# The shared expert's first matmuls, moved from the end of the expert loop to its middle, in a fused Mamba and mixture-of-experts layer

## The chip, the cores and the metric

The kernel runs on all 8 cores of one Trainium2 chip, one of the eight sequences on each, and the cores do not talk to each other. The metric is the device time of the slowest core in microseconds (us). Before the change it is 4697.62 us, the median of two runs (4684.04 and 4711.21).

## The reference

For each token row x (8 sequences of 4096 tokens, 1024 features) the layer computes

```python
xn = layernorm(x)
s  = mamba(xn)          # in_proj, causal conv, selective scan with 16 states, gate branch z, out_proj
g  = silu(moe(xn))      # 8 experts, top 2 by a sigmoid gate, plus one shared expert
out = x + s * g

# inside moe(xn)
h      = gelu(einsum('bsd,edh->bseh', xn, W1) + b1)          # experts, hidden width 512
y      = einsum('bseh,ehd->bsed', h, W2) + b2
shared = gelu(xn @ Ws1 + bs1) @ Ws2 + bs2                    # the same two steps, every token
return einsum('bse,bsed->bsd', gate_full, y) + shared

# inside mamba(xn): the recurrence over time
h_t = exp(delta_t * A) * h_{t-1} + delta_t * x_t * B_t
y_t = sum_n h_t[n] * C_t[n] + D * x_t
```

## The kernel before, in words

Each core walks over its sequence in 16 chunks of 256 tokens (`T = 256`). Features lie on partitions, tokens along the free dimension. Every weight matrix is turned to bf16 once in HBM; the weights of the experts, of in_proj, conv and out_proj are streamed in again for every chunk. Only the shared expert's weights stay in SBUF (`ws1_b`, `ws2_b`).

A small class, `Sched`, collects operations in program order, gives each to an engine, and derives the semaphore waits from named buffers that operations read and write. It reorders nothing: each engine does its own operations in the order in which the loop at the end of `build_nc` emits them. So the place of a call in that loop is its place in every engine's queue.

What belongs to the change:

- `scan_group(i, g)`, lines 804 to 842, does one eighth of the channels. VectorE multiplies u by B (`dBx`, L810). ScalarE computes 16 exponentials (`dA`, L817) into 7 slots, VectorE does 16 scans (`h_b`, L827), and frees a slot with each. Then VectorE multiplies by C (L839). ScalarE can be at most 7 exponentials ahead of the scans.
- `idents_phase(i, g)` sums the 16 states with 16 matmuls by an identity and one by a diagonal of D, into PSUM bank P7, and ScalarE copies the result to `y_b` (L866).
- `ffn_expert(i, e)` loads 2 x 512 KB of W1 and does 32 matmuls into banks P4 and P5 (`P<-xn_b,sb_w`). Four ScalarE activations with Gelu empty them into `scrb2` (L914).
- `hgate_phase(i, e)` multiplies by the gate on VectorE (L924).
- `ffn_w2(i, e)` loads 2 x 512 KB of W2 and does 32 matmuls into P0 to P3 (`P<-scrb,sb_w`). These banks add up over all experts.
- `ws1_phase(i)`, lines 870 to 887, is the shared expert's first half: 32 matmuls of the resident `ws1_b` with `xn_b` (`P<-xn_b,ws_b`), **also into P4 and P5**, emptied by four Gelu activations into `hsh` (L884). It loads nothing. `hsh` is read by the 32 matmuls `P<-hsh,ws_b` of `ffn_tail`.
- `out_proj_phase_b(i - 1)` does 16 matmuls of the previous chunk's out_proj (`P<-y_b,sb_out`), again into P4 and P5, and also P6 and P7. VectorE adds them to `s_f` (L501), `combine_phase` forms x + s * g (L508, L513), and `store_phase` transposes on TensorE (L526), copies on ScalarE (L534) and writes out from SyncE. Behind it come `ffn_tail`, the next chunk's load of x (`x_f`, L348) and its layernorm sums (`ln_stats`).

In a chunk, groups 0 and 1 of the scan are issued ahead of the expert loop, groups 2 to 5 in its iterations 0 to 3, and groups 6 and 7 in the next chunk. Iteration g does expert g, the state sum of group g, the W2 half of expert g - 1, the gate of expert g, and scan group g + 2. So on ScalarE the Gelu of expert 3 is followed by the 16 exponentials of group 5, and only behind those comes the Gelu of expert 4. Iterations 4 to 7 have no scan.

The loop reads (lines 1021 to 1031):

```python
for g in range(GD):
    ffn_expert(i, g)
    if g < GSPLIT:                 # GSPLIT = 6
        idents_phase(i, g)
    if g >= 1:
        ffn_w2(i, g - 1)
    hgate_phase(i, g)
    if g + 2 < GSPLIT:
        scan_group(i, g + 2)
ffn_w2(i, GD - 1)
ws1_phase(i)
```

and behind it, out_proj_phase_b, combine_phase and store_phase of chunk i - 1 and ffn_tail of chunk i.

Of the kernel before, what the change touches and what calls it, by code (L numbers as in the profile page):

```python
# [111 lines left out]
def build_nc(L):  # L112
# [51 lines left out]
    with ExitStack() as ctx:  # L164
# [86 lines left out]
        def apv(t_handle, offset, dims):  # L251
            base = t_handle[:, :] if t_handle.shape[0] == 128 else t_handle[0:t_handle.shape[0], :]
            return bass.AP(base.tensor, offset, [list(base.ap[0])] + [list(d) for d in dims])
# [3 lines left out]
        def mm(out_ap, lhsT, rhs, bank, first, last, reads, tag=""):  # L257
            def fn(eng, out_ap=out_ap, lhsT=lhsT, rhs=rhs, first=first, last=last):
                return eng.matmul(out_ap, lhsT, rhs, start=first, stop=last,  # L259
                                  skip_group_check=True)  # L260
            S.add("pe", fn, reads=tuple(reads), writes=(bank,), tag=tag)
# [542 lines left out]
        def scan_group(i, g):  # L804
            dpar = g % 2
            dko = dpar * 4096
            dk = "dBx:p%d" % dpar
            def fb(eng, g=g, dko=dko):
                u_bc = apv(sb["u_b"], g * 256, [[0, 16], [1, 256]])
                return eng.tensor_tensor(apv(sb["dBx"], dko, [[256, 16], [1, 256]]),  # L810
                                         u_bc, apv(sb["Bb"], 0, [[256, 16], [1, 256]]),
                                         ALU.mult)
            S.add("dve", fb, reads=("u:%d" % g, "Bb", dk), writes=(dk,), tag="dbx%d.%d" % (i, g))
            for n in range(DSTATE):
                slot = (g * DSTATE + n) % 7
                def fx(eng, g=g, n=n, slot=slot):
                    return eng.activation(sb["dA"][:, slot * 256:(slot + 1) * 256],  # L817
                                          sb["delta"][:, g * 256:(g + 1) * 256],
                                          AF.Exp, scale=sb["A_neg"][:, g * 16 + n:g * 16 + n + 1])
                S.add("act", fx, reads=("delta:%d" % g, "A_neg", "dA:s%d" % slot),  # L820
                      writes=("dA:s%d" % slot,), tag="ex%d.%d.%d" % (i, g, n))
                if n % 4 == 3:
                    for nn in range(n - 3, n + 1):
                        sl = (g * DSTATE + nn) % 7
                        def fsc(eng, g=g, nn=nn, sl=sl, i=i, dko=dko):
                            init = 0.0 if i == 0 else sb["carry"][:, g * 16 + nn:g * 16 + nn + 1]
                            return eng.tensor_tensor_scan(  # L827
                                sb["h_b"][:, nn * 256:(nn + 1) * 256],
                                sb["dA"][:, sl * 256:(sl + 1) * 256],
                                apv(sb["dBx"], dko + nn * 256, [[1, 256]]),  # L830
                                init, ALU.mult, ALU.add)
                        S.add("dve", fsc, reads=("dA:s%d" % sl, dk, "carry:g%d" % g, "h"),
                              writes=("h", "dA:s%d" % sl), tag="sc%d.%d.%d" % (i, g, nn))
            def fcs(eng, g=g):
                src = apv(sb["h_b"], 255, [[256, 16]])
                return eng.tensor_copy(sb["carry"][:, g * 16:(g + 1) * 16], src)
            S.add("dve", fcs, reads=("h",), writes=("carry:g%d" % g,), tag="cs%d.%d" % (i, g))
            def fhc(eng, dko=dko):
                return eng.tensor_tensor(apv(sb["dBx"], dko, [[256, 16], [1, 256]]),  # L839
                                         apv(sb["h_b"], 0, [[256, 16], [1, 256]]),  # L840
                                         apv(sb["Cb"], 0, [[256, 16], [1, 256]]), ALU.mult)
            S.add("dve", fhc, reads=("h", "Cb", dk), writes=(dk,), tag="hc%d.%d" % (i, g))
# [86 lines left out]
        def ffn_w2(i, e):  # L929
            par = e % 2  # L930
            for kh in range(2):
                spar = (e * 2 + kh) % 2
                def fld2(eng, e=e, kh=kh, spar=spar):
                    dst = sb["sb_w2"][:, spar * 2048:(spar + 1) * 2048].rearrange(
                        "p (kc d) -> p kc d", kc=2)
                    return eng.dma_start(out=dst, in_=blobs["blob_w2"][e, kh * 2:(kh + 1) * 2, :, :].rearrange("kc p d -> p kc d"))
                S.add("sp", fld2, reads=("blob_w2",), writes=("sbw2:p%d" % spar,),
                      dma="dw2" if spar == 0 else "dw2b", tag="ldw2%d.%d.%d" % (i, e, kh))
                for kci in range(2):
                    kc = kh * 2 + kci  # L940
                    for j in range(8):
                        bank = "P%d" % (j // 2)
                        half = (j % 2) * 256
                        lhsT = sb["sb_w2"][:, spar * 2048 + kci * 1024 + j * 128:
                                           spar * 2048 + kci * 1024 + (j + 1) * 128]
                        rhs = apv(sb["scrb1"], par * 1024 + kc * 256, [[1, 256]])
                        mm(ps[bank][:, half:half + 256], lhsT, rhs, bank,
                           e == 0 and kc == 0 and (j % 2 == 0), False,
                           ["sbw2:p%d" % spar, "scrb1:p%d" % par],
                           tag="w2_%d.%d.%d.%d" % (i, e, kc, j))  # L950
# [33 lines left out]
        for i in range(NCH + 1):  # L984
            if i < NCH:
                ln_xn(i)
            if i >= 1:
                scan_group(i - 1, GSPLIT)
                out_proj_phase_a(i - 1)
                out_proj_a_evac(i - 1, (6, 7, 4, 5, 0, 1, 2, 3))  # L990
            if i < NCH:
                in_proj_phase(i, 0)
            if i >= 1:
                scan_group(i - 1, GSPLIT + 1)
            if i < NCH:
                conv_phase(i, 0)
            if i >= 1:
                idents_phase(i - 1, GSPLIT, first=True)
            if i < NCH:
                gate_phase(i)  # L1000
                xproj_phase(i)
                bbcb_phase(i)
            if i >= 1:
                idents_phase(i - 1, GSPLIT + 1, first=True)
            if i < NCH:
                dt_phase(i)
                gate_bcast(i)
                scan_group(i, 0)
                in_proj_phase(i, 1)
                scan_group(i, 1)  # L1010
                conv_phase(i, 1)
                if i == 0:
                    late_setup_b()
                if DBG_CHUNK == i:
                    dbg_dump("dbg_xz", "xzh", "xzh")
                    dbg_dump("dbg_bb", "Bb", "Bb")
                    dbg_dump("dbg_cb", "Cb", "Cb")
                    dbg_dump("dbg_delta", "delta", "delta")
                    dbg_dump("dbg_u", "u", "u_b")
            if i < NCH:  # L1020
                for g in range(GD):
                    ffn_expert(i, g)
                    if g < GSPLIT:
# [3 lines that stand above are left out]
                    hgate_phase(i, g)  # L1027
                    if g + 2 < GSPLIT:
                        scan_group(i, g + 2)
                ffn_w2(i, GD - 1)  # L1030
                ws1_phase(i)
            if i >= 1:
                out_proj_phase_b(i - 1)
                combine_phase(i - 1)
                store_phase(i - 1)
            if i < NCH:
                ffn_tail(i)
                xz_tail_save(i, 0)
                xz_tail_save(i, 1)
                if i + 1 < NCH:  # L1040
                    prefetch(i + 1)
                    ln_stats(i + 1)
                if DBG_CHUNK == i:
                    dbg_dump("dbg_gf", "g", "g_f")
                    dbg_dump("dbg_hg", "scrb1:p1", "scrb1")
                    dbg_dump("dbg_gel", "scrb2:p1", "scrb2")
                    dbg_dump("dbg_ge", "ge_all", "ge_all")
# [96 lines left out]
```

How the kernel before makes its waits and increments, by code:

```python
                def run(eng):  # L1056
                    for op in S.ops:
                        if op["e"] != engine_name:
                            continue
                        for (s, v) in op["waits"]:
                            eng.wait_ge(sems[s], v)
                        inst = op["fn"](eng)
                        if getattr(S, "record", None) is not None:
                            try:
                                S.record.append((op["tag"], inst.ins.name))
                            except Exception:
                                pass
                        if op["inc"] is not None:
                            s, step = op["inc"]
                            inst.then_inc(sems[s], step)
                    if engine_name == "sp":
                        eng.wait_ge(sems["dst"], S.final.get("dst", 0))
```

## Time and profile before

| what | value |
|---|---|
| median of the runs | 4697.62 us (4684.04, 4711.21) |
| the profiled execution's own time | 4672.01 us |
| its span on core 0, the slowest | 4670.3 us |
| spans of the eight cores | 4638.8 to 4670.3 us |
| TensorE busy, matmuls | 2593.0 us (56%) |
| VectorE busy | 2489.9 us (53%) |
| ScalarE busy | 2113.8 us (45%) |
| mean granted TensorE clock of core 0 | 0.757 of full speed |

Read it as follows. No engine is busy for much more than half of the span, so the kernel is a chain of hand-overs rather than one full engine. The work repeats with each chunk, so the place to look is one chunk in the middle, in order of time. The profile names SBUF and PSUM tensors without their numbers: `P` is any PSUM bank, `sb_w` is `sb_w1` or `sb_w2`, `ws_b` is `ws1_b` or `ws2_b`, `scrb` is `scrb1` or `scrb2`.

### The profile page before, as it was taken

How to read it: one execution, taken by the hardware profiler on the slowest of the kernel's cores; microseconds unless marked ns; L12 is line 12 of the kernel's file. 1: busy time of each engine (PE TensorE's matmuls, PEld its weight loads, DVE VectorE, ACT ScalarE, POOL GpSimd, SP SyncE). 2: the span in 40 equal slices, each digit the busy share in tenths (PEclk: the TensorE clock that was granted, in tenths of full speed). 3: DMA queues.
4: the chain of work that ended last, by engine and by line, in shares of the span. 5: the costliest groups of instructions: out<-in, count | busy, mean ns of one | idle time of the engine just before them, and what ended most of it. 6: DMA issues, size and time to landing. Idle time of an engine off the chain costs nothing.

```text
span 4670.3 us, 72627 instructions; the slowest of 8 cores (4638.8 to 4670.3 us)
## 1 busy us (share of the span) xinstructions
PE 2593.0 (56%) x17792; PEld 1933.2 (41%) x17792; DVE 2489.9 (53%) x3013; ACT 2113.8 (45%) x4233; POOL 266.4 (6%) x386
## 2 busy tenths in 40 slices
PE   2104656565655656566565656656565565556555
PEld 1103535353543535344353534434353443445344
DVE  0205374554746455484645548464564846456484
ACT  1204363534536354453635445363544536354462
POOL 0100010101001010100101010010101001010100
PEclk6557877777787777778777877877787787878777
DMA  6794333333433333333333333333333333333332
GB/s 111 109 112 140 118 122 119 121 111 116 129 112 122 114 126 109 114 125 120 123 110 124 115 118 122 119 122 109 122 117 116 121 123 118 113 124 117 113 118 95
DMA packets 329940, 549.90 MB, mean 118 GB/s; under 512 B 20457, under 2 KB 170090, under 8 KB 324530
## 3 DMA queue, kind: packets, MB, share of 16 engines
q1 hardware_dynamic: 319554, 473.49, 31.6%
q0 software_dynamic: 9968, 71.77, 8.1%
q8 instruction: 148, 2.42, 0.2%
q14 instruction: 270, 2.21, 0.2%
HBM read 557.31 MB, written 46.47 MB: 129 GB/s over the span
## 4 chain that ended last, share of the span: by engine, by line
PE 29%; DVE 24%; DMA 15%; ACT 15%; issue 9%; another core or an unknown queue 5%; POOL 2%; DVEq 1%; ACTq 0%; SPq 0%; POOLq 0%
PE P L259 27%; DVE h_b L827 17%; DMA sb_in<-blob_in 5%; ACT scrb L914 3%; DMA sb_w<-blob_w 3%; DVE dBx L810 3%; DMA sb_out<-blob_out 3%; ACT L914 2%; ACT dA L817 2%; DMA x_f<-x_t 2%; ACT xzh L580 2%; POOL delta L697 1%; PE P L526 1%; DMA bc_dram<-bcB 1%
## 5 line engine op out<-in xcount | busy, mean ns | idle before, releaser
L827 DVE TENSOR_TENSOR_SCAN h_b<-dA,carry,dBx 128x256 bf16<-128x256 f32 x1920 | 1446.2, 753 | 651.2 <-ACT dA L817 424.3
L817 ACT ACTIVATE dA<-delta,A_neg 128x256 f32<-128x256 f32 x2048 | 947.4, 502 | 709.4 <-DVE h_b L827 705.4
L259 PE MATMUL P<-xn_b,sb_w 128*128 128x256 bf16 x4096 | 650.8, 329 | 739.9 <-ACT scrb L914 607.6
L259 PEld LDWEIGHTS P<-xn_b,sb_w 128*128 128x128 bf16 x4096 | 462.8, 116 | 924.7 <-issue 801.0
L259 PE MATMUL P<-scrb,sb_w 128*128 128x256 bf16 x4096 | 490.1, 279 | 48.4 <-DMA sb_w<-blob_w 48.2
L259 PEld LDWEIGHTS P<-scrb,sb_w 128*128 128x128 bf16 x4096 | 406.0, 100 | 114.9 <-issue 60.6
L810 DVE TENSOR_TENSOR dBx<-u_b,Bb 128x4096 bf16<-128x4096 bf16 x128 | 294.0, 2297 | 247.4 <-DMA Bb<-bc_dram 182.8
L914 ACT ACTIVATE scrb<-P,b1c 128x256 bf16<-128x256 f32 x512 | 242.4, 473 | 306.4 <-PE P L259 269.1
L259 PE MATMUL P<-xzh,sb_cd 128*128 128x256 bf16 x1024 | 199.8, 371 | 325.2 <-ACT xzh L580 153.8
L259 PE MATMUL P<-xn_b,sb_in 128*128 128x256 bf16 (+1 forms) x2176 | 292.1, 293 | 151.7 <-DMA sb_in<-blob_in 151.2
L924 DVE TENSOR_TENSOR scrb<-scrb,ge_all 128x1024 bf16<-128x1024 bf16 x128 | 88.4, 691 | 488.6 <-PE P L259 250.1
L259 PEld LDWEIGHTS P<-xn_b,sb_in 128*128 128x128 bf16 x2176 | 215.6, 107 | 225.4 <-issue 182.8
L839 DVE TENSOR_TENSOR dBx<-h_b,Cb 128x4096 bf16<-128x4096 bf16 x128 | 292.6, 2286 | 0.5 <-issue 0.5
L259 PEld LDWEIGHTS P<-xzh,sb_cd 128*128 128x128 bf16 x1024 | 124.3, 128 | 395.2 <-issue 353.6
L259 PE MATMUL P<-dBx,ident_b 128*128 128x256 bf16 x2048 | 271.0, 290 | 17.7 <-DVE dBx L839 16.8
L259 PEld LDWEIGHTS P<-dBx,ident_b 128*128 128x128 bf16 x2048 | 213.7, 105 | 58.9 <-issue 20.0
L668 POOL DMA_DIRECT2D bcB<-bc_f x16 | 8.0, 502 | 3936.3 <-ACT bcB L665 3936.3
L259 PE MATMUL P<-zc,sb_out 128*128 128x256 bf16 x1024 | 150.0, 314 | 111.3 <-DMA sb_out<-blob_out 111.3
L259 PE MATMUL P<-y_b,sb_out 128*128 128x256 bf16 x1024 | 162.2, 328 | 60.3 <-DMA sb_out<-blob_out 32.4
L259 PEld LDWEIGHTS P<-zc,sb_out 128*128 128x128 bf16 x1024 | 111.4, 112 | 150.5 <-issue 123.9
L501 DVE TENSOR_TENSOR s_f<-s_f,P 128x512 f32<-128x512 f32 x64 | 39.7, 682 | 234.7 <-PE P L259 234.7
L914 ACT ACT_TABLE_LOAD x80 | 102.6, 1283 | 131.4 <-PE P L259 130.0
(112 smaller groups left out, 2348.4 us busy)
## 6 DMA issues: line engine op xcount, KB each, us to landing
sb_w<-blob_w SPq DMA_DIRECT2D x512, 512.0 KB, 4.4
sb_in<-blob_in SPq DMA_DIRECT2D x256, 256.0 KB, 3.3
sb_out<-blob_out SPq DMA_DIRECT2D x128, 512.0 KB, 4.7
sb_cd<-blob_cd SPq DMA_DIRECT2D x128, 256.0 KB, 3.2
Bb<-bc_dram POOLq DMA_DIRECT2D x16, 1024.0 KB, 5.0
Cb<-bc_dram POOLq DMA_DIRECT2D x16, 1024.0 KB, 7.1
blob_w<-w_w POOLq DMA_DIRECT2D x2, 8192.0 KB, 121.8
out<-stage SPq DMA_DIRECT2D x32, 512.0 KB, 3.2
```

The source lines that it names most:

```text
L259: return eng.matmul(out_ap, lhsT, rhs, start=first, stop=last, skip_group_check=True)
L501: return eng.tensor_tensor(v, v, ps[bank][:, 0:512], ALU.add)
L526: return eng.matmul(bass.AP(ps[bank][:, :].tensor, gg * 128, [list(ps[bank][:, :].ap[0]), [1, 128]]), sb["s_f"][:, g * 256 + tb * 128: g * ...
L580: return eng.activation(dst, ps["P%d" % b][:, :].rearrange("p (b2 t) -> p b2 t", b2=2), AF.Copy)
L668: return eng.dma_start(out=sb["bcB"][32:48, :], in_=sb["bc_f"][16:32, :])
L697: return eng.tensor_tensor(d, d, scr, ALU.add)
L810: return eng.tensor_tensor(apv(sb["dBx"], dko, [[256, 16], [1, 256]]), u_bc, apv(sb["Bb"], 0, [[256, 16], [1, 256]]), ALU.mult)
L817: return eng.activation(sb["dA"][:, slot * 256:(slot + 1) * 256], sb["delta"][:, g * 256:(g + 1) * 256], AF.Exp, scale=sb["A_neg"][:, g * ...
L827: return eng.tensor_tensor_scan(sb["h_b"][:, nn * 256:(nn + 1) * 256], sb["dA"][:, sl * 256:(sl + 1) * 256], apv(sb["dBx"], dko + nn * 256 ...
L839: return eng.tensor_tensor(apv(sb["dBx"], dko, [[256, 16], [1, 256]]), apv(sb["h_b"], 0, [[256, 16], [1, 256]]), apv(sb["Cb"], 0, [[256, 1 ...
L914: return eng.activation(sb["scrb2"][:, par * 1024 + hg * 256: par * 1024 + (hg + 1) * 256], ps[bank][:, half:half + 256], AF.Gelu, bias=sb ...
L924: return eng.tensor_tensor(apv(sb["scrb1"], par * 1024, [[256, 4], [1, 256]]), apv(sb["scrb2"], par * 1024, [[256, 4], [1, 256]]), geb, AL ...
```

## The change

`ws1_phase(i)` is called in iteration 3 of the expert loop, after that iteration has issued scan group 5, and no longer behind the loop. Nothing else is edited: the same instructions are issued, with the same operands.

```diff
                     hgate_phase(i, g)
                     if g + 2 < GSPLIT:
                         scan_group(i, g + 2)
+                    if g == 3:
+                        ws1_phase(i)
                 ffn_w2(i, GD - 1)
-                ws1_phase(i)
             if i >= 1:
                 out_proj_phase_b(i - 1)
```

TensorE's queue from the W2 half of expert 2 to out_proj's phase b, in a chunk in the middle. Before (`xn_b,sb_w` is an expert's first half, `scrb,sb_w` a W2 half, `dBx,ident_b` and `xco,dd_b` a state sum, `xn_b,ws_b` the shared expert):

```order
L259 MATMUL P<-scrb,sb_w 128x256 x32
L259 MATMUL P<-xn_b,sb_w 128x256 x32
L259 MATMUL P<-dBx,ident_b 128x256 x16
L259 MATMUL P<-xco,dd_b 128x256
L259 MATMUL P<-scrb,sb_w 128x256 x32
L259 MATMUL P<-xn_b,sb_w 128x256 x32
L259 MATMUL P<-dBx,ident_b 128x256 x16
L259 MATMUL P<-xco,dd_b 128x256
L259 MATMUL P<-scrb,sb_w 128x256 x32
L259 MATMUL P<-xn_b,sb_w 128x256 x32
```

The same place after the change:

```order
L259 MATMUL P<-scrb,sb_w 128x256 x32
L259 MATMUL P<-xn_b,ws_b 128x256 x32
L259 MATMUL P<-xn_b,sb_w 128x256 x32
L259 MATMUL P<-dBx,ident_b 128x256 x16
L259 MATMUL P<-xco,dd_b 128x256
L259 MATMUL P<-scrb,sb_w 128x256 x32
L259 MATMUL P<-xn_b,sb_w 128x256 x32
L259 MATMUL P<-dBx,ident_b 128x256 x16
L259 MATMUL P<-xco,dd_b 128x256
L259 MATMUL P<-scrb,sb_w 128x256 x32
```

The shared expert's 32 matmuls stand ahead of expert 4, of the state sum of group 4 and of the W2 half of expert 3; they have left the place between the last W2 half and `P<-y_b,sb_out`.

ScalarE's queue at the same place, from the Gelu of expert 3 on. Before:

```order
L914 ACTIVATE scrb<-P,b1c 128x256 x4
L866 ACTIVATE y_b<-P 128x256
L817 ACTIVATE dA<-delta,A_neg 128x256 x16
L914 ACTIVATE scrb<-P,b1c 128x256 x4
L866 ACTIVATE y_b<-P 128x256
L914 ACTIVATE scrb<-P,b1c 128x256 x4
L866 ACTIVATE y_b<-P 128x256
L914 ACTIVATE scrb<-P,b1c 128x256 x8
L884 ACTIVATE hsh<-P,bs1c 128x256 x4
```

After:

```order
L914 ACTIVATE scrb<-P,b1c 128x256 x4
L866 ACTIVATE y_b<-P 128x256
L817 ACTIVATE dA<-delta,A_neg 128x256 x16
L884 ACTIVATE hsh<-P,bs1c 128x256 x4
L914 ACTIVATE scrb<-P,b1c 128x256 x4
L866 ACTIVATE y_b<-P 128x256
L914 ACTIVATE scrb<-P,b1c 128x256 x4
L866 ACTIVATE y_b<-P 128x256
L914 ACTIVATE scrb<-P,b1c 128x256 x8
```

The four activations that empty the shared expert's banks stand behind the 16 exponentials of scan group 5 and ahead of expert 4's Gelu. The queues of VectorE, GpSimd and SyncE are unchanged, so every DMA is issued in the same order as before.

## Rows read from the trace of the kernel before

**Rows 1.** The page, chain that ended last, shares of the span by line

```profile
PE P L259 27%; DVE h_b L827 17%; DMA sb_in<-blob_in 5%; ACT scrb L914 3%; DMA sb_w<-blob_w 3%; DVE dBx L810 3%; DMA sb_out<-blob_out 3%; ACT L914 2%; ACT dA L817 2%; DMA x_f<-x_t 2%; ACT xzh L580 2%; POOL delta L697 1%; PE P L526 1%; DMA bc_dram<-bcB 1%
```

**Rows 2.** Waits of TensorE over the span: us in total, times, longest us

```profile
PE P L259 <- ACT hsh L884: 28.5, 31, 1.3
```

**Rows 3.** Timeline, scan group 5: start us, us, engine, operation [idle before <-releaser]

```profile
1516.81 2.17 ACT L914 ACTIVATE scrb<-P,b1c 128x256 bf16<-128x256 f32 x4
...
1519.12 5.34 PE L259 MATMUL P<-xn_b,sb_w 128*128 128x256 bf16 x30 [0.44 <-ACT scrb L914]
...
1524.31 1.91 PE L259 MATMUL P<-dBx,ident_b 128*128 128x256 bf16 x16
...
1535.23 0.51 ACT L817 ACTIVATE dA<-delta,A_neg 128x256 f32<-128x256 f32 x1 [0.41 <-DVE h_b L827]
1535.76 1.28 ACT L914 ACT_TABLE_LOAD   x1
1537.05 2.17 ACT L914 ACTIVATE scrb<-P,b1c 128x256 bf16<-128x256 f32 x4
...
1538.34 0.58 PE L259 MATMUL P<-xn_b,sb_w 128*128 128x256 bf16 x2 [8.52 <-ACT scrb L914]
...
1539.37 5.46 PE L259 MATMUL P<-xn_b,sb_w 128*128 128x256 bf16 x30 [0.44 <-ACT scrb L914]
```

**Rows 4.** Timeline, TensorE behind expert 5: group 5's state sum and what follows

```profile
1544.66 1.91 PE L259 MATMUL P<-dBx,ident_b 128*128 128x256 bf16 x16
...
1546.52 3.66 PE L259 MATMUL P<-scrb,sb_w 128*128 128x256 bf16 x32
...
1550.01 3.67 PE L259 MATMUL P<-xn_b,sb_w 128*128 128x256 bf16 x32
```

**Rows 5.** Timeline, from the shared expert to the store

```profile
1572.44 3.67 PE L259 MATMUL P<-xn_b,ws_b 128*128 128x256 bf16 x32
1575.99 2.17 ACT L884 ACTIVATE hsh<-P,bs1c 128x256 bf16<-128x256 f32 x4 [12.18 <-PE P L259]
...
1577.28 0.38 PE L259 MATMUL P<-y_b,sb_out 128*128 128x256 bf16 x2 [1.17 <-ACT hsh L884]
...
1578.31 1.69 PE L259 MATMUL P<-y_b,sb_out 128*128 128x256 bf16 x14 [0.65 <-ACT hsh L884]
1579.45 2.48 DVE L501 TENSOR_TENSOR s_f<-s_f,P 128x512 f32<-128x512 f32 x4 [14.84 <-PE P L259]
...
1586.87 3.87 PE L526 MATMUL P<-ident_f,s_f 128*128 128x128 f32 x16 [6.87 <-DVE xzc L640]
...
1590.67 1.88 PE L259 MATMUL P<-gcm,b_b 8*128 8x256 bf16 x8
```

**Rows 6.** Tile hsh over the span: duration ns min/median/max, first and last start

```profile
L259 PE MATMUL P<-hsh,ws_b x512: 269/285/421, 500.0 to 4602.4; 128*128 128x256 bf16 x171
L884 ACT ACTIVATE hsh<-P,bs1c x64: 473/473/474, 497.6 to 4581.4; 128x256 bf16<-128x256 f32 x64
```

**Rows 7.** Timeline, TensorE: the 30 matmuls of expert 5 in two other chunks

```profile
1812.01 5.67 PE L259 MATMUL P<-xn_b,sb_w 128*128 128x256 bf16 x30 [0.44 <-ACT scrb L914]
...
3452.62 4.59 PE L259 MATMUL P<-xn_b,sb_w 128*128 128x256 bf16 x30 [0.44 <-ACT scrb L914]
```

**Rows 8.** Timeline, TensorE: waits for W2 in one chunk

```profile
4013.32 3.65 PE L259 MATMUL P<-scrb,sb_w 128*128 128x256 bf16 x32 [1.64 <-DMA sb_w<-blob_w]
...
4025.98 1.91 PE L259 MATMUL P<-scrb,sb_w 128*128 128x256 bf16 x16 [2.01 <-DMA sb_w<-blob_w]
```

**Rows 9.** Windows: us, busy by engine, granted clock, DMA share, GB/s

```profile
1545.00:1566.00 21.00, 19.33 (x176) 16.79 (x173) 2.08 (x3) 5.68 (x13) 0.00 (x0) 1.00 0.64 204
```

**Rows 10.** Timeline, TensorE entering the last W2 half, and phase b's load on SyncE

```profile
1565.80 0.42 SPq L483 DMA_DIRECT2D sb_out<-blob_out  x1
...
1567.25 3.00 PE L259 MATMUL P<-scrb,sb_w 128*128 128x256 bf16 x14 [2.00 <-DMA sb_w<-blob_w]
```

**Rows 11.** The page, DMA issues: KB each, median us from issue to landing

```profile
sb_out<-blob_out SPq DMA_DIRECT2D x128, 512.0 KB, 4.7
```

## The prediction, made before the changed kernel ran

> **What bounds the kernel now.** I read the chain that ended last first. It is spread over everything: TensorE's helper line has 27% of the span, the scans 17%, and no other line over 5% [rows 1]. So a per-engine average says nothing about moving one phase; what counts is which wait ends last at the two places of the change, in order of time. I take the chunk around 1500 to 1600 us; the others look alike.
>
> The first place is the middle of the expert loop [rows 3]. ScalarE finishes the Gelu of expert 3 at about 1519.0 and goes on to the 16 exponentials of scan group 5. They are paced by the scans, which free their slots, and the last starts at 1535.23. Then come a table load and the Gelu of expert 4 at 1537.05. TensorE meanwhile starts expert 4 (the 30 matmuls at 1519.12), the state sum of group 4 (1524.31) and, behind it, the W2 half of expert 3. Then it has nothing: it sits idle for 8.52 us, until the Gelu of expert 4 empties P4 and P5 and lets expert 5 in at 1538.34. So the time of scan group 5 is a hole for TensorE, into which three pieces of work fit, with 8.5 us to spare.
>
> The second place is the end of the loop. From 1544.66 TensorE is itself the chain: state sum 1544.66, W2 half 1546.52, expert 6 at 1550.01 [rows 4], and on to the shared expert at 1572.44. Over the window 1545 to 1566 its matmuls are busy for 19.33 of 21.00 us at a granted clock of 1.00, the higher of its two levels (2.4 GHz) [rows 9]. Behind the shared expert it waits for ScalarE to empty P4 and P5 into hsh, 1.17 and then 0.65 us, before out_proj's phase b; VectorE, idle for 14.84 us, waits for that phase; the transposes wait for VectorE [rows 5]. The wait on hsh is 28.5 us over the span, in 31 waits [rows 2].
>
> **What the change does, part by part.**
>
> *In the middle.* The shared expert's 32 matmuls have the shape of expert 4's and start when those did, at 1518 to 1519. They load nothing. They fill P4 and P5, and these banks are emptied only behind the exponentials of group 5: the four activations into hsh take the place of expert 4's Gelu, at 1537.05. Expert 4 needs the same two banks, so it starts where expert 5 started, at 1538.34. And in TensorE's queue two things stand behind the waiting expert 4 that do not need it: the state sum of group 4 and the W2 half of expert 3. Before, they ran in the hole; now they run after it. The hole grows from 8.5 to about 14 us and the work that was in it moves to the stretch in which TensorE is the chain.
>
> That TensorE does not let ready matmuls past waiting ones is seen in rows 5: the bias matmuls `P<-gcm,b_b`, whose inputs and banks P0 to P3 had long been ready, wait out the 6.87 us idle time behind the transposes and start at 1590.67. The Trainium skill says the same in "TensorE: Matmul & The Clock Gate", section "Step-by-step: what each phase is for": only weight loads are pulled ahead, the matmuls stay in program order. By that rule the change loses the hole; by the contrary reading, the last rival below, it would gain, and the trace speaks for the rule.
>
> So at 1544.66, where expert 5 ended before, expert 4 ends now. From there the list of before was: state sum, six expert blocks of 32 matmuls, shared expert. The list after is: two state sums and eight blocks. Added, at their starts in rows 4:
> - the state sum of group 4: 1546.52 - 1544.66 = 1.86
> - the W2 half of expert 3: 1550.01 - 1546.52 = 3.49
> - expert 5, now at full clock behind a running TensorE: another block, 3.49
> - together 8.84 us a chunk.
>
> *At the end.* Phase b ended at 1578.31 + 1.69 = 1580.00 [rows 5]. Without the shared expert and the wait for hsh it starts at 1572.44 and its 16 matmuls take 1.91, as 16 do at 1544.66 [rows 4]; it would end at 1574.35. Taken off: 5.65 us a chunk. Its own banks were emptied by expert 7's Gelu two blocks earlier, so that costs nothing.
>
> Net: 8.84 - 5.65 = **+3.19 us a chunk** at the end of phase b. What follows it (additions, combine, transposes, store, load of x, layernorm, the next in_proj) hangs on it in one chain and is shifted whole. That holds for 15 chunks: 47.9 us. The first chunk has no phase b. There the shared expert began at about 497.6 - 3.55 = 494.05 (3.55 us ahead of its first evacuation, as in rows 5) and the first matmul on hsh started at 500.0 [rows 6]; the 8 bias matmuls between them (1.88) stay, so 4.07 is saved and 8.84 added: +4.8. Sum 52.7 us.
>
> *Small terms, a chunk each.*
> - W2 and W1 loads. TensorE now streams two more blocks without a pause. A block takes 2 x 512 KB in 3.49 us, which is 300 GB/s; the window moved 204 GB/s at a DMA share of 0.64 [rows 9], so my estimate of the full rate is 204 / 0.64 = 319. That is close. One chunk shows a block held up by 1.64 us [rows 8]; rows 4 show none. Bounds 0 and 1.64; the stretches I saw mostly had waits near the lower end, so I take 0.3.
> - The Trainium skill ("DMA: Bandwidth & Descriptors", section "Where 436 GB/s comes from") gives about 358 GB/s as what HBM gives one core; by that figure this term would be 0, and the 1.64 us row disagrees.
> - The load for phase b. It is issued at 1565.80 and lands 4.7 us later by the median [rows 10, 11], at 1570.5, and is needed at 1572.44 instead of 1577.28. Bounds 0 and 0.9; I take 0.1, since 1.9 us of cover are left. If the W2 load ahead of it is late, so is the last block, which restores the cover.
> - Clock. Expert 4 follows an idle time of 14 us, not 8.52. Expert 5 has that place before; its 30 matmuls took 4.59 to 5.67 us in two other chunks [rows 7]; all at the lower level (3.00 / 14 = 0.214 us each [rows 10]) they would take 6.4, against 5.46 in rows 3. Bounds -0.9 and +1.0; I take 0, the value of rows 3.
> - Table loads. The first Gelu behind the exponentials pays 1.28 us, now the shared expert's and before expert 4's [rows 3]. Same count, 0. VectorE's gates are issued with slack of a whole block: 0.
>
> 0.4 x 16 = 6.4. **Sum: 52.7 + 6.4 = 59 us.** Against the profiled execution's own 4672.0 us that gives 4731. This execution was faster than both of the runs shown (4684.04, 4711.21; median 4697.62). The mean of the three is 4689, and I put the sum on that: **4748 us**. That is 1.3% over the level and 50 us over the median shown. About 2%, 94 us, can be told from no change.
>
> **The rivals.**
>
> *The weight stream breaks (slower by over 2%).* With two blocks more in a row at 300 of an estimated 319 GB/s, one more block per chunk waits as the last W2 half does: 2.00 us, and then 14 matmuls at 0.214 instead of 0.109 us, 1.5 us more [rows 10]. 3.5 x 16 = 56 on top of 59: 4804. For it: 1.64 and 2.01 us in one chunk [rows 8]. Against it: most blocks in rows 4 wait for nothing, and the moved state sum and W2 half find their weights and data long landed. It decides from 5.9 us a chunk, that is from 2.3 us of waits more than I count.
>
> *The end of the chunk is set by something else (no change).* If the loads behind phase b or the next chunk's scans bounded the chunk, 3 us of shift would be absorbed: 4689. For it: TensorE idles 6.87 us in this tail. Against it: in rows 5 each step starts when the one before ends, and VectorE's idle time of 14.84 us ends with TensorE.
>
> *Queued work gets past expert 4 (faster).* If the state sum and the W2 half ran in the hole after all, or the hsh activations got ahead of the exponentials, the middle would cost nothing and the end would save 5.65 x 15 + 4.1 = 89 us: 4600. It decides if expert 4 starts before 1535. Against it: the wait in rows 5 described above, and ScalarE's queue, in which hsh stands behind all 16 exponentials.
>
> **How the numbers follow.** Forecast 0.70, weight stream 0.16, no change 0.08, queued work gets past 0.04, 0.02 for the rest. For the forecast alone, -0.7 to +2.7 us a chunk around 3.19 gives 40 to 94 us, so 4712 to 4783 from the two levels 4672 and 4689. The range goes up to the stream's case, 4804, and leaves out the two faster ones. Slower by over 2%: 0.16. Faster by over 2%: 0.02, since even the full gain is 1.9%. Within 2%: 0.82.
>
> **What would show it.** Right: in a middle chunk the shared expert's matmuls start as the Gelu of expert 3 ends; TensorE is then idle for about 14 us until an hsh activation; the order behind it is expert 4, state sum, W2 half, expert 5 without a pause; phase b starts within 0.3 us of the last W2 half, with no wait on hsh; and the distance from one chunk to the next is 3 to 4 us longer. Wrong: waits on sb_w over 5 us a chunk in that stretch (the stream), an unchanged distance of the chunks (the tail absorbs it), or W2 matmuls of expert 3 ahead of expert 4.

## The result, and the profile after

| | before | after |
|---|---|---|
| median of the runs | 4687.18 us (10 runs) | 4742.93 us (11 runs) |
| ratio | | 1.0115, interval 1.0079 to 1.0151 |
| profiled execution, spans of the cores | 4638.8 to 4670.3 us | 4712.3 to 4741.5 us |

The changed kernel is slower by 1.15%, about 54 us, with an interval of 37 to 71 us. The forecast was 59 us on a level of 4689: 4748 us.

In some executions of either kernel four cores are granted a lower clock and take longer (in the profiled one after the change cores 0 to 3, 0.73 to 0.74 against 0.76), so the rows below are of core 6 (4718.2 us), and means of the changed kernel are of cores 4 to 7.

First the waits of TensorE by what ended them (us in total, times, longest). They answer to [rows 2]. Core 0 before the change:

```profile
PE P L259 <- ACT scrb L914: 607.6, 160, 9.1
PE P L259 <- DMA sb_w<-blob_w: 180.2, 43, 126.7
```

Core 6 after the change:

```profile
PE P L259 <- ACT scrb L914: 461.1, 128, 9.0
PE P L259 <- ACT hsh L884: 225.4, 32, 14.7
...
PE P L259 <- DMA sb_w<-blob_w: 195.8, 54, 125.9
```

The wait on hsh was 28.5 us in 31 waits of at most 1.3 us. It is now 225.4 us in 32 waits, the longest 14.7: two per chunk, a long one and a short one. This alone is not the loss. Most of it took the place of waits on the Gelu of expert 4 (607.6 us fell to 461.1), and idle time that another wait would have covered costs nothing. What counts is what ran in that idle time.

The timeline of the scan group shows that. It answers to [rows 3]: start us, us, engine, operation, and in brackets the idle time before it with its releaser.

```profile
1528.57 2.17 ACT L914 ACTIVATE scrb<-P,b1c 128x256 bf16<-128x256 f32 x4
...
1530.88 5.31 PE L259 MATMUL P<-xn_b,ws_b 128*128 128x256 bf16 x30 [0.55 <-ACT scrb L914]
...
1546.99 0.51 ACT L817 ACTIVATE dA<-delta,A_neg 128x256 f32<-128x256 f32 x1 [0.42 <-DVE h_b L827]
1547.51 1.28 ACT L884 ACT_TABLE_LOAD   x1
1548.81 2.17 ACT L884 ACTIVATE hsh<-P,bs1c 128x256 bf16<-128x256 f32 x4
...
1550.10 0.59 PE L259 MATMUL P<-xn_b,sb_w 128*128 128x256 bf16 x2 [13.90 <-ACT hsh L884]
...
1551.12 5.43 PE L259 MATMUL P<-xn_b,sb_w 128*128 128x256 bf16 x30 [0.44 <-ACT hsh L884]
```

Each row has its twin in [rows 3], with another name. The shared expert runs where expert 4 ran. The hsh activations stand where expert 4's Gelu stood, behind the last exponential and the table load. Expert 4 starts where expert 5 started. Only the idle time is longer, 13.90 us against 8.52 (over all chunks and cores 13.6 against 8.2 on average), and the state sum and the W2 half that used to run ahead of it are missing. They are in the next rows, which answer to [rows 4].

```profile
1556.39 1.91 PE L259 MATMUL P<-dBx,ident_b 128*128 128x256 bf16 x16
...
1561.74 3.67 PE L259 MATMUL P<-xn_b,sb_w 128*128 128x256 bf16 x32
...
1565.24 1.91 PE L259 MATMUL P<-dBx,ident_b 128*128 128x256 bf16 x16
...
1567.10 3.66 PE L259 MATMUL P<-scrb,sb_w 128*128 128x256 bf16 x32
```

From 1556.39 to 1565.24 TensorE does the state sum of group 4, the W2 half of expert 3 and expert 5: 8.85 us ahead of the state sum of group 5, with which this stretch began before.

The end of the loop answers to [rows 5].

```profile
1587.44 1.91 PE L259 MATMUL P<-scrb,sb_w 128*128 128x256 bf16 x16 [2.46 <-DMA sb_w<-blob_w]
...
1590.47 1.91 PE L259 MATMUL P<-scrb,sb_w 128*128 128x256 bf16 x16 [1.13 <-DMA sb_w<-blob_w]
...
1592.21 1.91 PE L259 MATMUL P<-y_b,sb_out 128*128 128x256 bf16 x16
1593.58 2.48 DVE L501 TENSOR_TENSOR s_f<-s_f,P 128x512 f32<-128x512 f32 x4 [9.25 <-PE P L259]
...
1600.99 3.87 PE L526 MATMUL P<-ident_f,s_f 128*128 128x128 f32 x16 [6.87 <-DVE xzc L640]
```

Out_proj's phase b follows the last W2 half without a wait. The transposes still wait 6.87 us for VectorE, as before, so the tail was moved and not changed.

A measure for the experiments follows from this: the time from the first matmul behind the last long wait on ScalarE (the row at 1538.34 in [rows 3], 1550.10 above) to the first transpose (1586.87 and 1600.99). Below it is called the end stretch. It is 48.5 us here before and 50.9 after. Means over the 13 chunks of the middle, worked out from the traces core by core:

| us | before, 8 cores | after, cores 4 to 7 |
|---|---|---|
| end stretch | 48.7 (48.3 to 49.2) | 51.8 (51.4 to 52.5) |
| of it waits on expert weights (`sb_w`) | 3.3 | 3.9 |
| rest of a chunk, from the transposes to the end of that wait | 224.1 (223.5 to 225.1) | 224.4 (224.0 to 224.7) |
| from one chunk's transposes to the next's | 272.8 (271.9 to 273.6) | 276.3 (276.1 to 276.4) |

A chunk is 3.5 us longer, and 3.2 of it are in the end stretch. Below, both measures are given as means over the cores of one profiled execution.

### The profile page after: what moved, and what is told of

Its sections match the earlier page's. It is cut to its first block, busy times and chain, and to the rows that moved or that the text cites. A ratio compares the mean times of both kernels' runs of the same rounds, so it can differ in the third digit from the quotient of the medians.

```text
span 4741.5 us, 72610 instructions; the slowest of 8 cores (4712.3 to 4741.5 us)
## 1 busy us (share of the span) xinstructions
PE 2644.1 (56%) x17792; PEld 1968.0 (42%) x17792; DVE 2492.3 (53%) x3013; ACT 2115.8 (45%) x4233; POOL 266.1 (6%) x386
## 4 chain that ended last, share of the span: by engine, by line
PE 31%; DVE 23%; DMA 15%; ACT 14%; issue 8%; another core or an unknown queue 5%; POOL 2%; DVEq 1%; ACTq 0%; SPq 0%; POOLq 0%
PE P L259 30%; DVE h_b L827 16%; DMA sb_in<-blob_in 4%; DMA sb_w<-blob_w 3%; DVE dBx L810 3%; DMA sb_out<-blob_out 3%; ACT scrb L914 2%; DMA x_f<-x_t 2%; ACT dA L817 2%; ACT L914 2%; ACT xzh L580 2%; POOL delta L697 1%; DMA bc_dram<-bcB 1%; PE P L526 1%
## 5 line engine op out<-in xcount | busy, mean ns | idle before, releaser
L259 PE MATMUL P<-xn_b,sb_w 128*128 128x256 bf16 x4096 | 637.4, 326 | 665.6 <-ACT scrb L914 306.1
L259 PEld LDWEIGHTS P<-xn_b,sb_w 128*128 128x128 bf16 x4096 | 461.1, 115 | 835.2 <-issue 716.0
L259 PE MATMUL P<-scrb,sb_w 128*128 128x256 bf16 x4096 | 509.5, 286 | 50.3 <-DMA sb_w<-blob_w 50.0
L259 PEld LDWEIGHTS P<-scrb,sb_w 128*128 128x128 bf16 x4096 | 415.9, 102 | 125.3 <-issue 61.2
L259 PE MATMUL P<-dBx,ident_b 128*128 128x256 bf16 x2048 | 282.6, 298 | 17.4 <-DVE dBx L839 16.5
L534 ACT ACTIVATE stage<-P 128x512 f32<-128x512 f32 x64 | 38.2, 598 | 370.9 <-PE P L526 302.0
L259 PE MATMUL P<-xn_b,ws_b 128*128 128x256 bf16 x512 | 95.3, 365 | 136.1 <-ACT scrb L914 136.1
```

Source lines behind the costliest of these rows:

```text
L534: return eng.activation(sb["stage"][:, gq * 512:(gq + 1) * 512], ps[bank][:, :], AF.Copy)
```

## The experiments

Each is an edit of one of the two kernels. They ran in three groups, each on one chip, and "before" was run again beside each group, with a median of 4678 to 4682 us. So kernels of different groups are compared by their ratios to it.

### Only the state sum ahead of expert 4

```diff
 # changed kernel
-                    ffn_expert(i, g)
+                    if g != 4:
+                        ffn_expert(i, g)
                     if g < GSPLIT:
                         idents_phase(i, g)
+                    if g == 4:
+                        ffn_expert(i, g)
```

> The changed kernel, with the state sum of group 4 issued ahead of expert 4, so that it runs while expert 4 waits for the hsh activations; the W2 half of expert 3 stays behind. Theory (what stands behind the blocked expert 4 is lost, 1.86 us for the state sum a chunk): 16 x 1.86 = 30 us faster than the changed kernel, so about 4713 where the kernel before is at 4687 (+0.55%). Rival, weight stream (the loss is waits on weights in the longer stretch): the stretch has as many streamed blocks and one pause less, so no gain, 4743 or a little more. Rival, the tail absorbs: no change from 4743 either.

Measured: 4705.75 us, ratio 1.0061 (1.0018 to 1.0103) to the kernel before; the theory said 1.0055. The end stretch is 50.2 us, 1.6 less than after the change, and a chunk takes 274.2 us, 2.1 less. TensorE in one chunk, core 2:

```profile
1528.28 1.91 PE L259 MATMUL P<-dBx,ident_b 128*128 128x256 bf16 x16
1530.03 0.27 PE L259 MATMUL P<-xco,dd_b 128*128 128x256 bf16 x1
1542.23 0.59 PE L259 MATMUL P<-xn_b,sb_w 128*128 128x256 bf16 x2 [11.93 <-ACT hsh L884]
```

One piece of work of 1.86 us, moved past the blocked expert, gives about its own length back. The rivals expected nothing. The intervals of the two ratios overlap (1.0079 to 1.0151 for the changed kernel), so by the times alone this step is not certain; the traces show it.

### State sum and W2 half ahead of expert 4

```diff
 # changed kernel
-                    ffn_expert(i, g)
+                    if g not in (4, 5):
+                        ffn_expert(i, g)
                     if g < GSPLIT:
                         idents_phase(i, g)
+                    if g == 5:
+                        ffn_expert(i, g)
                     if g >= 1:
                         ffn_w2(i, g - 1)
+                    if g == 4:
+                        ffn_expert(i, g)
```

> The changed kernel, with the state sum of group 4 and the W2 half of expert 3 both issued ahead of expert 4, and the state sum of group 5 between experts 4 and 5. Theory: of the 8.84 us a chunk that were added only expert 5's block of 3.49 is left, against 5.65 saved at the end: -2.16 us a chunk for 15 chunks and about -0.6 in the first, so 33 us faster than the kernel before, about 4654 (-0.7%), and 86 us faster than the changed kernel. The wait of expert 5 for expert 4's Gelu (about 1.5 us) lies beside the state sum of group 5. Rival, weight stream: the W1 loads of expert 5 are now needed right behind expert 4, so waits on sb_w rise by 1 to 2 us a chunk and the time is 4670 to 4700.

Measured: 4672.20 us, ratio 0.9989 (0.9967 to 1.0011). That is 1.2% below the changed kernel, some 60 us by the ratios, where 86 were expected. And it only equals the kernel before, where the sum said 0.7% less. Here the rival about the weight stream was partly right. Waits of TensorE, core 6, and expert 5 in one chunk:

```profile
PE P L259 <- DMA sb_w<-blob_w: 227.8, 79, 128.0
```

```profile
1544.84 0.27 PE L259 MATMUL P<-xco,dd_b 128*128 128x256 bf16 x1
...
1545.98 1.93 PE L259 MATMUL P<-xn_b,sb_w 128*128 128x256 bf16 x16 [0.86 <-DMA sb_w<-blob_w]
...
1549.99 1.91 PE L259 MATMUL P<-xn_b,sb_w 128*128 128x256 bf16 x16 [2.08 <-DMA sb_w<-blob_w]
```

Without the one long wait in the first chunk (128.0) the waits on expert weights are 99.8 us on this core. On all eight cores they are 75 to 100 us, on average 89; in the kernel before they are 53 to 68 us, on average 58. The 30 us between the averages are nearly the whole shortfall against the expected 33 us of gain. Experts 4 and 5 follow each other here with only a state sum between them, and 2.94 us of waits appear in this chunk.

### The same, with expert 5's W1 in a free buffer

```diff
 # kernel ahead_both, in ffn_expert
+                wt, wkeys, wsem = "sb_w1", ("sbw1:p%d" % spar,), ...
+                if e == 5:
+                    wt, wkeys, wsem = "sb_in", ("sbin:p%d" % (2 * kh), "sbin:p%d" % (2 * kh + 1)), ("din", "din1")[kh]
```

> The kernel ahead_both, with expert 5's W1 loaded into sb_in (free in the loop) and not into sb_w1, so that both halves are fetched while TensorE waits for scan group 5. It asks why ahead_both came out 28 us slower than its sum. Theory (two expert blocks follow each other there, and each half of sb_w1 is refilled only once the half before it is used up, 4 us too late): the two waits on sb_w behind the state sum of group 5, 0.86 and 2.08 us in the chunk looked at, are gone, 2 to 3 us a chunk: 32 to 46 us faster than ahead_both, 1% below the kernel before. Rival, the 16 DMA engines are full in this stretch, and the same bytes are waited for somewhere later: less than 10 us of gain.

Measured: 4652.08 us, ratio 0.9945 (0.9913 to 0.9977). It is 20 us below ahead_both by the medians (expected 32 to 46). The two waits are gone:

```profile
1533.58 1.91 PE L259 MATMUL P<-dBx,ident_b 128*128 128x256 bf16 x16
1535.33 0.27 PE L259 MATMUL P<-xco,dd_b 128*128 128x256 bf16 x1
1535.44 3.94 PE L259 MATMUL P<-xn_b,sb_in 128*128 128x256 bf16 x32
1539.22 3.66 PE L259 MATMUL P<-scrb,sb_w 128*128 128x256 bf16 x32
```

On core 4, the one shown, waits on sb_w fall to 192.5 us, of which 128.4 is the first chunk's. The end stretch falls from 48.3 to 46.5 us and a chunk from 272.4 to 270.4 us, which is 2.0 a chunk or 32 us. By the trace the theory has its size; by the medians it has less than two thirds of it, and the two intervals overlap, so I leave it at "most". The rival (full DMA engines, the wait comes back later) expected less than 10 us. That it failed does not say why the load was late in ahead_both: its second half of W1 was issued at 1543.34 and landed 6.51 us later, with two loads of W2 issued within 1.4 us behind it, while the quickest load of this stretch (issued at 1569.02) landed in 3.53 us. A late refill and shared DMA engines both fit that, and an earlier refill cures both.

### The shared expert at both places

```diff
 # changed kernel
                 ffn_w2(i, GD - 1)
+                ws1_phase(i)
```

> The shared expert's first half at both places, in iteration 3 and behind the loop; it is computed twice with the same result. This gives the price in the middle alone. Theory: 8.84 us a chunk, 16 chunks, 141 us, and some 10 us of waits on weights: about 4838 (+3.2%). Rival, the tail absorbs the shift: under 4750. Rival, weight stream as the main cost: waits on sb_w over 5 us a chunk more than before, and any total.

Measured: 4841.21 us, ratio 1.0341 (1.0304 to 1.0378), 160 us. On cores 0 to 3 (clock 0.76) the end stretch is 57.5 us, 8.8 more than before, of which 0.4 are waits on weights (3.7 against 3.3). The middle costs what was worked out, and all of it reaches the end: a chunk takes 282.6 us, 9.8 more. The last 1.0 of these lies outside the end stretch, and these runs do not say what it is. The rival in which the tail absorbs the shift is excluded.

### The shared expert's first half left out

```diff
 # kernel before; leaves out the first matmul and the Gelu of the shared expert
                 ffn_w2(i, GD - 1)
-                ws1_phase(i)
+                if i == 0:
+                    S.add("gp", lambda eng: eng.memset(sb["hsh"][:, :], 0.0),
+                          reads=(), writes=("hsh",), tag="hsh0")
```

> The kernel before with the shared expert's first half left out (its 32 matmuls and 4 activations; hsh is set to zero once). This gives the saving at the end alone, which is also what the work costs at its old place. Theory: 5.65 us a chunk for 15 chunks and 4.1 in the first, 89 us: about 4598 (-1.9%). Rival, something else ends the chunk: -20 us or less.

Measured: 4607.25 us, ratio 0.9854 (0.9816 to 0.9893), so 68 us and not 89. In the profiled execution cores 4 to 7 took 4597 to 4614 us at a clock of 0.70 to 0.72, cores 0 to 3 took 4557 to 4573 at 0.76. The latter are 81 to 103 us below their own spans before, on average 89. On these cores the end stretch is 42.8 us, 5.8 less than before, and a chunk 5.9 less, where 5.65 was expected. In one of the four executions all eight cores had a clock of 0.755 to 0.765, and it took 4585.72 us, 92 us below the median of before. So the saving at the end is right in size, and the smaller ratio goes with the clock of the other cores.

### Split into two pieces, in a bank that nobody waits for

```diff
 # kernel before
                     ffn_expert(i, g)
+                    if g in (3, 5):
+                        ws1_half_evac(i, (g - 3) // 2)   # 2 Gelu activations, P6 -> hsh
                     if g < GSPLIT:
                         idents_phase(i, g)
                     if g >= 1:
                         ffn_w2(i, g - 1)
+                    if g in (2, 4):
+                        ws1_half(i, (g - 2) // 2)        # 16 matmuls into P6
                     hgate_phase(i, g)
...
                 ffn_w2(i, GD - 1)
-                ws1_phase(i)
```

> The shared expert's first half in two pieces of 16 matmuls, both into bank P6, which nothing uses in the loop: the first behind the W2 half of expert 1 (emptied behind expert 3's Gelu), the second behind the W2 half of expert 3 (emptied behind expert 5's Gelu). Both pieces lie in idle time of TensorE, and no expert waits for their bank. Theory (the change costs only because expert 4 shares P4 and P5 and drags what stands behind it): nothing is added in the middle, 5.65 us a chunk is saved at the end, so 80 to 89 us faster than the kernel before, -1.7 to -1.9%. Rival, work in the hole costs in itself (the clock, SBUF or PSUM traffic beside the scans): less than half of that gain. Rival, weight stream: waits on sb_w rise as in the changed kernel, 10 to 20 us of the gain lost.

Measured: 4584.68 us, ratio 0.9784 (0.9750 to 0.9817): 2.2% faster than before, 3.3% faster than the changed kernel. TensorE in one chunk, core 0:

```profile
1512.39 1.91 PE L259 MATMUL P<-dBx,ident_b 128*128 128x256 bf16 x16
1514.14 0.27 PE L259 MATMUL P<-xco,dd_b 128*128 128x256 bf16 x1
1514.25 3.66 PE L259 MATMUL P<-scrb,sb_w 128*128 128x256 bf16 x32
1517.74 1.92 PE L259 MATMUL P<-xn_b,ws_b 128*128 128x256 bf16 x16
1526.14 0.59 PE L259 MATMUL P<-xn_b,sb_w 128*128 128x256 bf16 x2 [6.48 <-ACT scrb L933]
```

State sum and W2 half are back in the hole, the second piece of the shared expert (`xn_b,ws_b`) stands behind them, and 6.48 us of the hole are left over; before it was 8.52. This is the move that the change wanted. The end stretch is 42.9 us and a chunk takes 266.9 us, the same as with the work left out (42.8 and 266.9): here the shared expert's first half costs nothing. Neither the clock nor traffic beside the scans takes anything back that the trace would show. The gain by the times, 94 to 101 us, is a little over the 80 to 89 expected; 5.9 us in each of 16 chunks are 94.

### The two lines swapped

```diff
 # changed kernel
-                    if g + 2 < GSPLIT:
-                        scan_group(i, g + 2)
                     if g == 3:
                         ws1_phase(i)
+                    if g + 2 < GSPLIT:
+                        scan_group(i, g + 2)
```

> The changed kernel with the two lines swapped: in iteration 3 the shared expert is issued ahead of scan group 5, so its four activations stand ahead of the 16 exponentials and not behind them. It still uses P4 and P5. Theory (it is ScalarE's order that holds the banks): expert 4 starts about 8 us later than in the kernel before but still runs inside the hole, with the state sum and W2 half behind it; the exponentials start 7.4 us later than before, of which some 6 us are slack because VectorE has the products and the gate of expert 3 to do first, so 1.1 us a chunk are added and 5.65 saved: about 71 us faster than the kernel before, -1.5%. Rival, it is the place in TensorE's queue alone that costs: as slow as the changed kernel, +1.1%. Rival, the scans have no slack: 7.4 us added, 1.8 us a chunk slower than before, +0.6%.

Measured: 4600.78 us, ratio 0.9838 (0.9795 to 0.9882): 1.6% faster than before. The same two calls in the other order make 142 us between the medians of this kernel and the changed one, and 2.8%, 130 us, between their ratios. In the kernel before ScalarE begins the exponentials here:

```profile
1520.57 2.91 ACT L817 ACTIVATE dA<-delta,A_neg 128x256 f32<-128x256 f32 x7
```

Core 7 of this kernel, the order on ScalarE and the first scans of group 5:

```profile
1499.45 2.18 ACT L914 ACTIVATE scrb<-P,b1c 128x256 bf16<-128x256 f32 x4
...
1501.77 4.81 PE L259 MATMUL P<-xn_b,ws_b 128*128 128x256 bf16 x30 [0.55 <-ACT scrb L914]
...
1506.46 2.18 ACT L884 ACTIVATE hsh<-P,bs1c 128x256 bf16<-128x256 f32 x4 [4.56 <-PE P L259]
1507.59 2.29 DVE L810 TENSOR_TENSOR dBx<-u_b,Bb 128x4096 bf16<-128x4096 bf16 x1 [0.52 <-issue]
1507.76 0.38 PE L259 MATMUL P<-xn_b,sb_w 128*128 128x256 bf16 x2 [1.17 <-ACT hsh L884]
...
1509.96 4.53 ACT L817 ACTIVATE dA<-delta,A_neg 128x256 f32<-128x256 f32 x11
...
1510.57 3.32 DVE L827 TENSOR_TENSOR_SCAN h_b<-dA,carry,dBx 128x256 bf16<-128x256 f32 x4 [0.69 <-ACT dA L817]
```

In TensorE's queue the shared expert stands exactly where the change put it. Only its activations come first on ScalarE, and expert 4 waits 1.17 us for them instead of 13.90. ScalarE idles 4.56 us for the matmuls, and still the first scan is held up by only 0.69 - 0.17 = 0.52 us in this chunk (0.17 is the usual gap), since VectorE was busy with its products until 1509.88. That is the smallest value of this core. Over all chunks and cores the idle time ahead of this scan is 1.5 us on average, against 0.2 before, so the hold-up is 1.3 us a chunk, where 1.1 was expected. A chunk takes 267.9 us, 4.9 less than before and 1.0 more than in the split kernel. The exponentials start 10.5 us after expert 3's Gelu (1499.45 to 1509.96); before, it was 3.8 (1516.81 to 1520.57).

### Split, and the last expert's W2 in a free buffer

```diff
 # kernel split_p6, in ffn_w2
+                wt, wkeys, wsem = "sb_w2", ("sbw2:p%d" % spar,), ...
+                if e == 7:
+                    wt, wkeys, wsem = "sb_in", ("sbin:p%d" % (2 * kh), "sbin:p%d" % (2 * kh + 1)), ("din", "din1")[kh]
```

> The kernel split_p6, with the last expert's W2 loaded into sb_in and not into sb_w2. It asks what the wait of 2 us ahead of the last W2 half is, and whether a version beats both kernels further. Theory (a W2 half follows a W2 half, and sb_w2 is refilled only once it is used up): the wait and the one behind it, some 3 us a chunk, are gone: 40 to 50 us faster than split_p6, -3% against the kernel before. Rival, full DMA engines: the wait moves to another load, less than 15 us.

Measured: 4539.45 us, ratio 0.9703 (0.9673 to 0.9732): 45 us below split_p6 by the medians and 38 by the ratios, 3.0% below the kernel before and the fastest of all. A chunk takes 264.5 us, 2.4 less than in split_p6, which is 38 us too. Waits of TensorE (core 6), and the end of the loop:

```profile
PE P L259 <- DMA sb_w<-blob_w: 145.1, 28, 126.0
```

```profile
1520.09 3.66 PE L259 MATMUL P<-scrb,sb_w 128*128 128x256 bf16 x32
1523.58 3.66 PE L259 MATMUL P<-scrb,sb_in 128*128 128x256 bf16 x32
1527.07 1.91 PE L259 MATMUL P<-y_b,sb_out 128*128 128x256 bf16 x16
```

19.1 us of waits on sb_w are left outside the first chunk, against 60.7 in split_p6 (185.9 less 125.2); over eight cores 15 on average against 60. So the waits around the last W2 half were a refill that could not start earlier. The kernel before shows the same: its first load for the last W2 half was issued at 1563.59, as the half-buffer came free, landed after 3.5 us, at 1567.12, and TensorE started at 1567.25.

## Why the prediction was right

**What was right.** 4748 us was forecast, 4742.93 measured; 59 us slower against 54.
- *The shared expert takes expert 4's place, and hsh the place of its Gelu.* Seen row by row above. The idle time of "about 14 us" is 13.90, and 13.6 on average.
- *Added 8.84 us a chunk.* 8.85 in the chunk shown; 8.8 in the end stretch of the kernel that does the work twice, 9.8 in its whole chunk.
- *Taken off 5.65 us.* 5.8 in the kernel without the work, by the end stretch of cores 0 to 3.
- *3 to 4 us from chunk to chunk.* The distance grew by 3.5 us, where 3.19 and 0.4 had been summed up. In the first chunk, from the last long wait to the first matmul on hsh, it is 5.1 us more (45.4 against 40.3), where 4.8 was forecast.
- *What stands behind the blocked expert is the loss.* Shown by two undoings: the state sum gives back 1.6 to 2.1 us a chunk, both pieces together a ratio of 0.9989 in place of 1.0115. TensorE did not let the ready state sum pass expert 4 in any chunk of any core (in 128 of 128 the first matmul behind the long wait is expert 4's), so the Trainium skill's statement that matmuls stay in program order ("TensorE: Matmul & The Clock Gate", section "Step-by-step: what each phase is for") agrees with the 13.90 us in which it did not start one.
- *The clock costs nothing more.* The 30 matmuls of expert 4 behind 13.90 us of idle time took 5.43 us; expert 5's took 5.46 behind 8.52. Over all chunks and cores it is 5.37 us behind 13.6 and 5.40 behind 8.2. Here the longer idle time does not make a slower start.
- *Phase b's load stays covered.* No wait on sb_out ahead of phase b (1592.21).
- *Everything behind phase b is shifted whole.* The rest of the chunk is 224.4 us against 224.1. The twice and dropped kernels exclude that something else ends the chunk.

**What was off in size.** Little that these runs can tell. The term for the weight loads was 0.3 us a chunk. The waits on sb_w without the first chunk's are 58 us on average before (53 to 68 on the eight cores) and 67 on cores 4 to 7 after (62 to 71), which is 0.5 a chunk; over all eight cores it is 0.2. The forecast of 59 us came out 5 us over the ratio's 54, whose interval reaches from 37 to 71, and the spans of the profiled executions differ by 58 us (4656.8 on average before, 4715.1 on cores 4 to 7 after). So no term is shown to be too high. That the level of 4689, a mean of three executions 39 us apart, came within 2 us of the later median was luck in part.

The rows for this term hold two kinds of waits, which the prediction did not tell apart. The load behind the 1.64 us wait was issued at 4006.51, under 4 us behind the two W1 loads, and took 6.67 us to land. TensorE was ready for it at 4011.68, so 3.5 us would have been in time: this load was slow and not late. The loads behind the waits of 2.00 and 2.01 us, ahead of the last W2 half, took only 3.5 us (1563.59 to 1567.12, 4022.30 to 4025.84): they were quick and issued late.

**The rivals.** The weight stream did not break in the changed kernel: the rows from 1556.39 to 1567.10 show no wait on weights. I put that down to the moved W2 half, whose weights had long landed, and to the second state sum, which is a pause; this is argued and not tested. It did bite in ahead_both, where I had put it as the rival and not in the sum: two W1 halves in a row. "Queued work gets past expert 4" did not happen in any chunk, but its price, 89 us, was about right: it is what a kernel gains that gives the waiting work another bank (0.9784) or lets ScalarE empty the bank first (0.9838).

## What to carry to other kernels

Idle time of an engine is only worth filling with work that blocks nothing behind it: before moving a phase into a hole, ask which buffer it holds, which instruction empties that buffer, and what stands ahead of that instruction on its engine. Here the hole was real and the work fitted (the split version costs nothing for it), but its bank was emptied only behind 16 paced exponentials, and an in-order queue made everything behind the next user of the bank wait too. And when two phases of the same kind are put next to each other, look at how early their buffers can be refilled.

## What the runs showed that I had not expected

- The order of two calls, scan group and shared expert, is worth 130 us by the ratios (1.0115 against 0.9838), more than moving the phase at all. ScalarE's exponentials can start some 7 us late at the price of 1.3 us, because VectorE's own gate and multiplication come first.
- I had estimated the stretch as close to the full DMA rate (300 of 319 GB/s). Most of the waits in it, those around the last W2 half, were nevertheless a matter of when a buffer is free: with one refill moved to a free buffer, 41.6 us of 60.7 vanished while the bytes moved stayed the same. The estimate of 319 GB/s from a mean share was too low as a limit. In the fastest kernel 10 us of this stretch moved 320 GB/s at a share of 0.92 (core 6; the last three numbers are clock, share and GB/s):

```profile
1514.00:1524.00 10.00, 9.14 (x84) 7.95 (x83) 1.07 (x2) 1.89 (x4) 0.00 (x0) 1.00 0.92 320
```
